# Cross attention: the weighing of key blocks 0 to 9 done two blocks at a time, and the maxima slots dealt out anew

## The chip, the cores and the metric

The kernel runs on one core of a Trainium2 chip. The metric is the device time of one execution in microseconds (us). The core has a matrix engine (TensorE, in profile rows PE, its weight loads PEld), a vector engine (VectorE, DVE), a scalar engine (ScalarE, ACT), a general engine (GpSimd, POOL) and a queue engine (SyncE, SP). Each works through its own list of instructions in order, and they wait for each other by semaphores.

## The reference

A decoder layer on x of 4 x 1024 x 512: self attention over 2048 fixed keys, cross attention over 1601 context rows with 16 heads of 32, and a feed-forward part with 8 experts. The change lies in the cross attention alone. Cut to that:

```python
q = _split_heads(Q @ Wq_w.T + Wq_b)
k = _split_heads(K @ Wk_w.T + Wk_b)
v = _split_heads(V @ Wv_w.T + Wv_b)
scores = jnp.einsum('bhqd,bhkd->bhqk', q, k) / np.sqrt(DK).astype(np.float32)
scores = jnp.where(mask == 0, jnp.float32(-1000000000.0), scores)
attn = jax.nn.softmax(scores, axis=-1)
out = jnp.einsum('bhqk,bhkd->bhqd', attn, v)
```

The softmax needs, for each query and head, the maximum of its scores over all 1601 keys.

## The kernel before

The cross attention is cut into 32 units: 4 batches x 4 groups of 4 heads x 2 halves of 512 queries. A unit goes through 13 key blocks (`kt` 0 to 12, 128 keys each, the last 65). Keys stand on the partitions and queries along the free dimension, so the maximum over keys can't be had from these scores. It is found one unit ahead in a second product with queries on the partitions: 64 slots a unit, each one matmul of 402 keys (`mx`, L1579, which calls L1096) into one of three PSUM banks (`mx_ps`), and one VectorE read of that bank that adds the mask and takes the maximum (`read`, L1756 on, which calls L1103). Slot n may be written once slot n-3 has been read: TensorE waits on `mx_read` ahead of every slot, VectorE on `mx_made`.

TensorE's order is written out by hand in `unit`. In block `kt` it makes the scores of block `kt`+1, for two pairs of heads (`score`, L1594, two matmuls; `add_mask`, L1600, one each), with slots strewn between; then two more slots; then it weighs block `kt` (`weigh`, L1608): the probabilities times the values, four heads at once in four column tiles of the array (32 columns each), two passes each, so 8 matmul records; then what is left of the block's slots. `SLOTS_OF` says how many slots each block has: blocks 0 to 8 share all 64. In block 9 (`TURN`) the finished maxima are turned by TensorE (L1584), copied by ScalarE and sent through DRAM into the next unit's queries as one more row. In block 12 TensorE also starts the sum of the probabilities (column tiles again, L1608 into `xa_mx_ps`), and behind block 12 `add_up` adds VectorE's and GpSimd's share of it.

ScalarE takes the exponential of each pair's scores (L1726); the scores of a pair may be overwritten once that is done, and block n's exponential goes into a ring of four places, so it waits until block n-4 has been weighed. GpSimd adds the probabilities of blocks 0 to 8 (L1561), VectorE those of 9 to 11 behind its 64 reads (L1778), then the reciprocal (L1782) and the product (L1786). The last of the 32 units has no slots, as no unit follows it.

Of the kernel before, what the change touches and what calls it, by code (L numbers as in the profile page):

```python
# [592 lines left out]
KT = (S2 + P - 1) // P  # L593
# [466 lines left out]
RING = 4  # L1060
# [334 lines left out]
def cross_attention(nc, ident, ident_b, kT, qT, v, mask_q, mask_t, row, oT, first, queries_1, probs, any_key, outputs, Wo, bo, x1):  # L1395
# [7 lines left out]

    HALF = S // BANK
    units = B * GROUPS * HALF
    SLOTS_OF = [2, 7, 8, 8, 8, 8, 8, 8, 7] + [0] * (KT - 9)
    SLOT_OF = [sum(SLOTS_OF[:n]) for n in range(KT + 1)]
    assert SLOT_OF[KT] == SLOTS
    TURN = 9
    OWN = {"pool": tuple(range(9)), "dve": (9, 10, 11)}  # L1410
    OWN_LAST = {"pool": tuple(range(5)), "dve": tuple(range(5, 12))}
    POOL_ADDS, DVE_ADDS = len(OWN["pool"]) - 1, len(OWN["dve"])
    FIRST_STORED = GROUPS * HALF
# [3 lines left out]
    with ExitStack() as ctx:  # L1417
# [8 lines left out]
        unread, maxima, neg_max, max_row = first.unread, first.maxima, first.neg_max, first.max_row  # L1426
# [31 lines left out]
        def keys_of(kt):  # L1458
            return LAST if kt == KT - 1 else P

        def wait_added(eng, u, kt, own):

            if kt < 0:
                u, kt, own = u - 1, kt + KT, OWN
            if kt == KT - 1:
# [32 lines left out]
        with nc.Block() as block:  # L1498
# [53 lines left out]
            def _(pool):  # L1552
# [5 lines left out]
                def add(u, kt, left, right):  # L1558
                    for pr in range(PAIRS):
                        pool.wait_ge(exped, PAIRS * (KT * u + kt) + pr + 2 + PAIRS)  # L1560
                        pool.tensor_tensor(sums[pr][:, :, :], left[pr][:, :, :],  # L1561
                                           right[pr][:, :, :], ALU.add).then_inc(pool_added, 1)

                def unit(u, par, half, at, more):
                    pool.wait_ge(total_made, u + 2)
                    add(u, 1, prob[at], prob[(at + 1) % RING])
                    own = OWN if more else OWN_LAST
                    for n, kt in enumerate(own["pool"][2:]):
# [7 lines left out]
            def _(pe):  # L1576
                def mx(u, par, half, slot):
                    m = SLOTS * u + slot
                    pe.wait_ge(mx_read, m + 2)  # L1579
                    scores_of_slot(pe, mx_ps[slot % 3], qp[par], kp[par], half, slot).then_inc(mx_made, 1)  # L1580

                def turn_peaks(u):
                    pe.wait_ge(peaks, u + 3)
                    pe.transpose(peak_ps[0:GH * QB, 0:P], neg_max[:, :], ident[:, :]).then_inc(row_made, 1)  # L1584

                def score(u, par, half, kt, pr):
                    keys = keys_of(kt)
                    if kt == 0 and pr == 0:
                        pe.wait_ge(row_in, 16 * (u + 1))
                    queries = slice(half * BANK, (half + 1) * BANK)  # L1590
                    pe.wait_ge(exped, PAIRS * (KT * u + kt - 1) + pr + 2 + PAIRS)
                    for jj in range(2):
                        j = 2 * pr + jj
                        pe.matmul(scores[pr][0:keys, jj, :], kp[par][0:ROWS97, j, kt * P:kt * P + keys],  # L1594
                                  qp[par][0:ROWS97, j, queries], start=True, stop=False)
# [9 lines left out]
                def four_heads(total, left, right, start, stop):  # L1605
                    for j in range(GH):
                        mine = slice(j * DK, (j + 1) * DK)
                        last = pe.matmul(total[mine, :], left(mine), right[j // 2][0:left(mine).shape[0], j % 2, :],  # L1608
                                         start=start, stop=stop, tile_position=(0, j * DK))
                    return last  # L1610

                def weigh(u, par, kt, ring):
                    keys = keys_of(kt)
                    if kt == 0:
                        pe.wait_ge(o_kept, u + 2)
                    pe.wait_ge(exped, PAIRS * (KT * u + kt + 1) + 1 + PAIRS)
                    if kt == KT - 1:
                        pe.wait_ge(sum_kept, u + 2)
                        four_heads(sum_ps, lambda mine: ones[0:keys, :], prob[ring], True, False)
                    four_heads(o_ps, lambda mine: vg[par][0:keys, kt, mine], prob[ring],  # L1620
                               kt == 0, kt == KT - 1).then_inc(weighed, 1)
# [30 lines left out]
                def unit(u, par, half, at, more):  # L1652
                    nxt = (par if half == 0 else 1 - par, 1 - half)
                    for kt in range(KT):
                        slots = iter(range(SLOT_OF[kt], SLOT_OF[kt + 1]) if more else ())

                        def maxima(most):
                            for slot in itertools.islice(slots, most):
                                mx(u + 1, *nxt, slot)

                        following = (u, par, half, kt + 1) if kt + 1 < KT else (u + 1, *nxt, 0) if more else None
                        between = 1 if kt else 0
                        for pr in range(PAIRS) if following else ():
                            score(*following, pr)
                            if pr == 1:
                                maxima(between)
                            add_mask(following[2], following[3], pr, 0)
                            if pr == 0:
                                maxima(between)
                            add_mask(following[2], following[3], pr, 1)  # L1670
                            if pr == 0:
                                maxima(between)
                        if more and kt == TURN:
                            turn_peaks(u + 1)
                        maxima(2 * between)
                        weigh(u, par, kt, (at + kt) % RING)
                        if more and kt == 0:
                            pe.wait_ge(row_kept, u + 3)
                            pe.wait_ge(sum_kept, u + 2)
                            if half == 1:  # L1680
                                pe.wait_ge(loaded, 16 * (LOADS * (u // HALF + 1)))
                        maxima(SLOTS_OF[kt])
                        if not more and kt < DC:
                            turn_output_weight(kt)
                    add_up(u, OWN if more else OWN_LAST)

# [13 lines left out]
            def _(act):  # L1700
# [28 lines left out]
                def unit(u, par, half, at, more):  # L1729
                    for kt in range(KT):  # L1730
                        if kt + 1 < KT:
                            exp(u, kt + 1, (at + kt + 1) % RING, OWN if more else OWN_LAST)
                        elif more:
                            exp(u + 1, 0, (at + KT) % RING, OWN)
                        if more and kt == TURN:
                            keep_row(u + 1)
# [1264 lines left out]
```

## Time and profile before

| what | value |
|---|---|
| median of 3 runs | 3894.85 us (3888.32 to 3895.75) |
| the profiled execution | span 3891.2 us |
| TensorE busy | 3788.4 us (97%) |
| VectorE busy | 2395.0 us (62%) |
| ScalarE busy | 1432.7 us (37%) |
| GpSimd busy | 1534.5 us (39%) |
| cross attention, from its first to its last unit | about 1288 to 3015 us |

The profiled execution gives only its span, from its first to its last instruction; no time of its own around the span is given, and the span lies between the lowest and the median of the runs, 3.7 us below the median. Times in rows are us from the span's start. Matmuls are pipelined: a busy TensorE is not one at its peak. The granted TensorE clock is 1.00 over the cross attention.

### The profile page before, as it was taken

The page shows a single profiled execution, that of the slowest core. Times are in us where ns is not written, and L with a number is a line of the kernel's source. Part 1 is how long each engine was busy: PE and PEld are TensorE (multiplying, and loading weights), DVE is VectorE, ACT ScalarE, POOL GpSimd, SP SyncE. Part 2 cuts the span into 40 slices and gives each one's busy share as a digit, 9 for nine tenths or more (in the row PEclk, how much of TensorE's full clock was granted, in tenths as well). Part 3 has the DMA queues.
Part 4 walks back from the last instruction along what each step waited for, and adds up shares of the span by engine and source line. Part 5 has one row for each costly group of instructions (what it writes and reads, how often), then busy time and mean ns, then how long its engine had stood idle before and what let it go on. Part 6 is the DMA issues. An engine that isn't in the chain of part 4 may idle for free. (4 is left out here: it accounts for less than half of the span.)

```text
span 3891.2 us, 63669 instructions
## 1 busy us (share of the span) xinstructions
PE 3788.4 (97%) x19001; PEld 2532.2 (65%) x19161; DVE 2395.0 (62%) x6222; ACT 1432.7 (37%) x1793; POOL 1534.5 (39%) x860
## 2 busy tenths in 40 slices
PE   8999999999999899999999999999999999999998
PEld 7888888888877444544444444544444777777776
DVE  6544444444458688888888788878887533433135
ACT  3111222233224455455545555445555221222332
POOL 1000000000013667766677666766665222312234
PEclk9999999999999999999999999999999999999999
DMA  4001000145555322222112222222111433328579
GB/s 157 32 32 32 32 32 32 44 172 178 191 179 186 94 57 55 57 57 46 35 38 57 58 57 58 54 57 55 33 36 49 151 126 132 114 92 278 185 263 332
DMA packets 223177, 381.89 MB, mean 98 GB/s; under 512 B 17544, under 2 KB 102056, under 8 KB 222892
## 3 DMA queue, kind: packets, MB, share of 16 engines
q1 hardware_dynamic: 192876, 301.34, 26.7%
q0 software_dynamic: 14752, 49.29, 3.5%
q10 hardware_dynamic: 15264, 27.79, 1.9%
q8 instruction: 137, 2.24, 0.2%
q14 instruction: 148, 1.21, 0.1%
HBM read 229.71 MB, written 148.66 MB: 97 GB/s over the span
## 5 line engine op out<-in xcount | busy, mean ns | idle before, releaser
L1103 DVE CUSTOM_DVE_ANT_0 xf_unread<-xa_mx_ps,mask_q 128x402 bf16<-128x402 f32 x1984 | 1036.0, 573 | 290.3 <-PE xa_mx_ps L1096 156.7
L1726 ACT ACTIVATE probs<-xa_scores 128x1024 f32<-128x1024 f32 (+1 forms) x416 | 417.5, 1024 | 417.0 <-PE xa_scores L1600 371.6
L1726 ACT ACTIVATE xa_probs<-xa_scores 128x1024 f32<-128x1024 f32 (+1 forms) x416 | 417.3, 1024 | 397.8 <-PE xa_scores L1600 355.1
L1561 POOL TENSOR_TENSOR xa_sums<-xa_sums,xa_probs 128x1024 f32<-128x1024 f32 x220 | 519.7, 2383 | 18.1 <-POOL xa_sums L1561 15.7
L1561 POOL TENSOR_TENSOR xa_sums<-xa_sums,probs 128x1024 f32<-128x1024 f32 x220 | 519.3, 2381 | 18.9 <-POOL xa_sums L1561 15.3
L1600 PE MATMUL xa_scores<-mask_t,ident_b 128*128 128x512 bf16 (+1 forms) x1505 | 499.7, 387 | 5.3 <-issue 0.2
L1096 PE MATMUL xa_mx_ps<-xa_kp,queries 96*128 96x402 f32 x1024 | 364.2, 418 | 0.8
L1096 PE MATMUL xa_mx_ps<-xf_kp,queries 96*128 96x402 f32 x960 | 341.5, 418 | 0.4
L1594 PE MATMUL xa_scores<-queries,xf_kp 97*128 97x512 f32 (+1 forms) x832 | 284.2, 423 | 16.3 <-ACTq L1748 8.2
L1096 PEld LDWEIGHTS xa_mx_ps<-xa_kp,queries 96*128 96x128 f32 x1024 | 181.7, 189 | 172.2 <-DVE xf_maxima L1103 111.6
L1594 PE MATMUL xa_scores<-queries,xa_kp 97*128 97x512 f32 (+1 forms) x832 | 284.7, 423 | 1.8 <-ACT probs L1726 1.8
L1600 PEld LDWEIGHTS xa_scores<-mask_t,ident_b 128*128 128x128 bf16 (+1 forms) x1664 | 122.9, 100 | 244.7 <-issue 212.0
L253 POOL TENSOR_TENSOR sa_rstd<-sa_var,sa_power 128x1 f32<-128x1 f32 x32 | 17.7, 552 | 662.6 <-DVE sa_var L440 662.6
L1096 PEld LDWEIGHTS xa_mx_ps<-xf_kp,queries 96*128 96x128 f32 x960 | 170.4, 189 | 157.1 <-DVE xf_maxima L1103 98.3
L386 ACT ACTIVATE sa_pT_high<-sa_pT_ps 128x512 fp32r<-128x512 f32 x128 | 73.1, 597 | 534.1 <-PE sa_pT_ps L305 534.1
L44 PE MATMUL sa_o_ps<-sa_v_high,sa_pT_high 128*128 128x512 f32 x512 | 209.3, 409 | 3.0 <-DVE sa_pT_low L465 3.0
L44 PE MATMUL sa_scores<-weights,sa_nT_high 128*128 128x512 f32 x512 | 204.4, 399 | 1.4 <-DVE sa_nT_low L448 1.4
L46 PE MATMUL sa_scores<-weights,sa_nT_low 128*128 128x512 f32 x512 | 203.2, 397 | 0.0
L1594 PEld LDWEIGHTS xa_scores<-queries,xf_kp 97*128 97x128 f32 (+1 forms) x832 | 148.8, 187 | 83.5 <-ACT xa_probs L1726 26.0
L45 PE MATMUL sa_scores<-queries,sa_nT_high 128*128 128x512 f32 x512 | 202.6, 396 | 0.0
L46 PE MATMUL sa_o_ps<-sa_v_high,sa_pT_low 128*128 128x512 f32 x512 | 201.2, 393 | 0.0
L45 PE MATMUL sa_o_ps<-sa_v_low,sa_pT_high 128*128 128x512 f32 x512 | 199.8, 390 | 0.0
(415 smaller groups left out, 7388.0 us busy)
## 6 DMA issues: line engine op xcount, KB each, us to landing
bridge_rows<-sorted_in SPq DMA_DIRECT2D x78, 256.0 KB
sorted_out<-ex_made ACTq DMA_DIRECT2D x78, 256.0 KB
queries<-qT_high SPq DMA_DIRECT2D x30, 512.0 KB
xf_kp<-kT_high SPq DMA_DIRECT2D x16, 800.5 KB, 12.4
xa_kp<-kT_high SPq DMA_DIRECT2D x16, 800.5 KB
rows<-in_ctx SPq DMA_DIRECT2D x16, 768.0 KB, 5.1
values<-cxl_v SPq DMA_DIRECT2D x48, 256.0 KB
kT_high<-cxl_kT_high SPq DMA_DIRECT2D x12, 768.0 KB, 4.0
```

What stands on the lines that cost most here:

```text
L44: pe.matmul(out, lh, rh, start=start, stop=False)
L45: pe.matmul(out, lh, rl, start=False, stop=False)
L46: return pe.matmul(out, ll, rh, start=False, stop=stop)
L253: pool.tensor_tensor(rstd[:, :], var[:, :], power[:, :], ALU.pow).then_inc(root, 1)
L386: act.activation(pT[0][:, j * KB:(j + 1) * KB, :], pT_ps[j % 2][:, :, :], ACT.Copy).then_inc(pT_high, 1)
L1096: return pe.matmul(out[:, 0:MKEYS], qp[0:MAXROW, j, first:first + P], kp[0:MAXROW, j, MFIRST[kb]:MFIRST[kb] + MKEYS], start=True, stop=True)
L1103: return dve.tensor_tensor_reduce(out=unread[slot % 2][:, :], in0=scores[:, 0:MKEYS], in1=mask_q[:, half * QB + qt, MFIRST[kb]:MFIRST[kb] ...
L1561: pool.tensor_tensor(sums[pr][:, :, :], left[pr][:, :, :], right[pr][:, :, :], ALU.add).then_inc(pool_added, 1)
L1594: pe.matmul(scores[pr][0:keys, jj, :], kp[par][0:ROWS97, j, kt * P:kt * P + keys], qp[par][0:ROWS97, j, queries], start=True, stop=False)
L1600: last = pe.matmul(scores[pr][0:keys, jj, :], ident_b[0:keys, 0:keys], mask_t[0:keys, kt, queries], start=False, stop=True)
L1726: act.activation(prob[ring][pr][0:keys, :, :], scores[pr][0:keys, :, :], ACT.Exp, scale=SCALE).then_inc(exped, 1)
```

## The change

Two things change, both in the order of TensorE's instructions; no instruction of the computation is added or left out.

- Blocks 0 to 9 are no longer weighed in their own block, but in twos in the odd block: 0 and 1 in block 1, and so on to 8 and 9 in block 9. Blocks 10, 11 and 12 stay as they were. The waits at the head of `weigh` go with it, the wait for `o_kept` from block 0 to block 1.
- The slots are dealt 3, 8, 7, 9, 7, 9, 7, 9, 5 instead of 2, 7, 8, 8, 8, 8, 8, 8, 7, and the second pair's two mask products have a slot between them, as the first pair's already had.

```diff
@@ -1403,10 +1403,11 @@
     HALF = S // BANK
     units = B * GROUPS * HALF
-    SLOTS_OF = [2, 7, 8, 8, 8, 8, 8, 8, 7] + [0] * (KT - 9)
+    SLOTS_OF = [3, 8, 7, 9, 7, 9, 7, 9, 5] + [0] * (KT - 9)
...
     TURN = 9
+    WEIGHED_AT = {1: (0, 1), 3: (2, 3), 5: (4, 5), 7: (6, 7), 9: (8, 9), 10: (10,), 11: (11,), 12: (12,)}
@@ -1665,15 +1666,15 @@
                             if pr == 1:
                                 maxima(between)
                             add_mask(following[2], following[3], pr, 0)
-                            if pr == 0:
-                                maxima(between)
+                            maxima(between)
                             add_mask(following[2], following[3], pr, 1)
                             if pr == 0:
                                 maxima(between)
                         if more and kt == TURN:
                             turn_peaks(u + 1)
                         maxima(2 * between)
-                        weigh(u, par, kt, (at + kt) % RING)
+                        for due in WEIGHED_AT.get(kt, ()):
+                            weigh(u, par, due, (at + due) % RING)
```

What that does to TensorE's list stands at two places. The first is the end of block 0, between the last mask product of block 1's scores and the first slots (`xa_mx_ps` is a slot's bank, `xa_o_ps` the weighed sum). Before:

```order
L1600 MATMUL xa_scores<-mask_t,ident_b 128x512 x2
L1615 REGISTER_ALU
L1616 ISA [waits xa_o_kept]
L1608 MATMUL xa_o_ps<-probs,xf_vg 32x512 [waits xa_exped]
L1608 MATMUL xa_o_ps<-probs,xf_vg 32x512 x3
L1678 REGISTER_ALU
L1579 ISA [waits xa_sum_kept,xa_row_kept]
L1096 MATMUL xa_mx_ps<-xf_kp,queries 128x402 [waits xa_mx_read]
```

Now:

```order
L1601 MATMUL xa_scores<-mask_t,ident_b 128x512 x2
L1679 REGISTER_ALU
L1680 REGISTER_ALU [waits xa_row_kept]
L1580 ISA [waits xa_sum_kept]
L1096 MATMUL xa_mx_ps<-xf_kp,queries 128x402 [waits xa_mx_read]
```

The weighing of block 0 is gone from here, so a unit's first slot stands right behind the scores. The second place is the weighing in block 3, with the slots ahead of it and behind. Before:

```order
L1096 MATMUL xa_mx_ps<-xf_kp,queries 128x402 [waits xa_mx_read]
L1616 ISA
L1608 MATMUL xa_o_ps<-xa_probs,xf_vg 32x512 [waits xa_exped]
L1608 MATMUL xa_o_ps<-xa_probs,xf_vg 32x512 x3
L1579 REGISTER_ALU
L1096 MATMUL xa_mx_ps<-xf_kp,queries 128x402 [waits xa_mx_read]
```

Now:

```order
L1096 MATMUL xa_mx_ps<-xf_kp,queries 128x402 [waits xa_mx_read]
L1617 REGISTER_ALU
L1609 MATMUL xa_o_ps<-xa_probs,xf_vg 32x512 [waits xa_exped]
L1609 MATMUL xa_o_ps<-xa_probs,xf_vg 32x512 x3
L1617 ISA
L1609 MATMUL xa_o_ps<-xa_probs,xf_vg 32x512 [waits xa_exped]
L1609 MATMUL xa_o_ps<-xa_probs,xf_vg 32x512 x3
L1580 REGISTER_ALU
L1096 MATMUL xa_mx_ps<-xf_kp,queries 128x402 [waits xa_mx_read]
```

Two weighings, of blocks 2 and 3, now stand back to back between two slots; block 2 has slots alone.

## Rows read from the trace of the kernel before

**Rows 1.** The page: engines; costliest groups (busy, mean ns, idle before, releaser).

```profile
span 3891.2 us, 63669 instructions
PE 3788.4 (97%) x19001; PEld 2532.2 (65%) x19161; DVE 2395.0 (62%) x6222; ACT 1432.7 (37%) x1793; POOL 1534.5 (39%) x860
L1103 DVE CUSTOM_DVE_ANT_0 xf_unread<-xa_mx_ps,mask_q 128x402 bf16<-128x402 f32 x1984 | 1036.0, 573 | 290.3 <-PE xa_mx_ps L1096 156.7
```

**Rows 2.** Windows of one unit: its slots' reads, then the rest.

```profile
core 0: us, PE busy (x) PEld busy (x) DVE busy (x) ACT busy (x) POOL busy (x), PEclk, DMA share, GB/s
1562.27:1599.62 37.35, 37.16 (x192) 20.31 (x195) 33.48 (x128) 16.46 (x17) 36.03 (x16) 1.00 0.00 1
1599.62:1612.20 12.58, 12.51 (x77) 4.11 (x76) 11.34 (x11) 8.46 (x10) 0.37 (x1) 1.00 0.00 1
```

**Rows 3.** VectorE's timeline in block 8 of that unit (start, us).

```profile
1597.02 0.58 DVE L1103 CUSTOM_DVE_ANT_0 xf_unread<-xa_mx_ps,mask_q 128x402 bf16<-128x402 f32 x1
...
1597.52 0.57 DVE L1103 CUSTOM_DVE_ANT_0 xf_unread<-xa_mx_ps,mask_q 128x402 bf16<-128x402 f32 x1
...
1598.62 0.58 DVE L1103 CUSTOM_DVE_ANT_0 xf_unread<-xa_mx_ps,mask_q 128x402 bf16<-128x402 f32 x1 [0.51 <-issue]
```

**Rows 4.** TensorE's timeline in block 5 of the unit before.

```profile
1526.56 0.63 PE L1594 MATMUL xa_scores<-queries,xf_kp 97*128 97x512 f32 x2
...
1528.85 0.75 PE L1096 MATMUL xa_mx_ps<-xf_kp,queries 96*128 96x402 f32 x2
1529.53 1.06 PE L1608 MATMUL xa_o_ps<-probs,xf_vg 128*32 128x512 f32 x8
1530.53 0.82 PE L1096 MATMUL xa_mx_ps<-xf_kp,queries 96*128 96x402 f32 x3
1531.18 0.63 PE L1594 MATMUL xa_scores<-queries,xf_kp 97*128 97x512 f32 x2
```

**Rows 5.** TensorE's timeline, from block 12 of one unit into block 0 of the next.

```profile
1555.88 1.06 PE L1608 MATMUL xa_mx_ps<-probs,xa_ones 65*32 65x512 f32 x8
1556.76 1.04 PE L1608 MATMUL xa_o_ps<-probs,xf_vg 65*32 65x512 f32 x8
1557.62 1.04 PE L1608 MATMUL xa_mx_ps<-xa_sums,xa_ones 128*32 128x512 f32 x8
1558.59 0.73 PE L1594 MATMUL xa_scores<-queries,xf_kp 97*128 97x512 f32 x2
...
1560.09 0.61 PE L1600 MATMUL xa_scores<-mask_t,ident_b 128*128 128x512 bf16 x2
1560.62 1.07 PE L1608 MATMUL xa_o_ps<-probs,xf_vg 128*32 128x512 f32 x8
1561.62 0.64 PE L1096 MATMUL xa_mx_ps<-xa_kp,queries 96*128 96x402 f32 x2
```

**Rows 6.** TensorE's timeline from block 8 to the unit's end.

```profile
1597.99 0.63 PE L1096 MATMUL xa_mx_ps<-xa_kp,queries 96*128 96x402 f32 x2
...
1600.29 0.27 PE L1584 MATMUL xa_mx_ps<-ident,xf_neg_max 128*16 128x128 f32 x1
1600.49 1.06 PE L1608 MATMUL xa_o_ps<-xa_probs,xf_vg 128*32 128x512 f32 x8
1601.48 0.73 PE L1594 MATMUL xa_scores<-queries,xf_kp 97*128 97x512 f32 x2
...
1612.18 0.72 PE L1594 MATMUL xa_scores<-queries,xa_kp 97*128 97x512 f32 x2
```

**Rows 7.** ScalarE's timeline in block 7 of that unit.

```profile
1596.70 1.03 ACT L1726 ACTIVATE xa_probs<-xa_scores 128x1024 f32<-128x1024 f32 x1 [0.33 <-PE xa_scores L1600]
```

**Rows 8.** VectorE's timeline behind the unit's reads.

```profile
1599.73 0.22 DVE L1768 TENSOR_REDUCE xf_neg_max<-xf_maxima 128x16 f32<-128x64 f32 x1
...
1610.92 0.69 DVE L1786 TENSOR_TENSOR any_key<-xa_o_sb,xa_sum_sb 128x512 f32<-128x512 f32 x1
```

**Rows 9.** Line 1584 over the whole trace, one instruction a unit with slots.

```profile
L1584 PE MATMUL xa_mx_ps<-ident,xf_neg_max x31: 272/273/273, 1330.1 to 2957.7; 128*16 128x128 f32 x31
```

## The prediction

> **What bounds the kernel now.** I read the page first: TensorE is busy 97% of the span [rows 1], which would say that anything that shortens its work shortens the kernel. But a matmul that waits or drains counts as busy, so I went to one unit. The windows [rows 2] part it into the stretch in which VectorE reads the 64 slots (37.35 us) and the rest (12.58 us, no slots). TensorE looks full in both. The timeline of VectorE [rows 3] shows how the first stretch is paced. Reads that follow each other at once start 0.50 us apart (1597.02, 1597.52). The next one starts 1.10 us later, at 1598.62: that is 0.60 us in which VectorE had nothing to read, and it lies beside a weighing. So 64 reads take 64 x 0.50 = 32.0 us, and 37.35 - 32.0 = 5.35 us are gaps. Eight weighings lie in the stretch (blocks 1 to 8); 8 x 0.60 = 4.8 us, nearly all of it.
>
> The reason is the three banks. While TensorE weighs it makes no slots; VectorE lives on what lies in the banks, at most three reads, partly used up when the weighing starts.
>
> Is TensorE or VectorE the limit there? TensorE's prices, from its timelines: of a block's four score and four mask products the first six take 1558.59 to 1560.09 [rows 5], 1.50 us; 0.10 of that is getting out of the weighing before (two score products behind a weighing show 0.73 us, elsewhere 0.63 [rows 4, 5]), so one takes 0.233 and eight 1.87 us. The weighing starts 0.53 us after the last two began, 0.06 more than they need: getting into the column tiles. Three slots take 1530.53 to 1531.18 with the 0.10 in it, 0.18 to 0.19 each [rows 4]. A lone weighing then costs 1561.62 - 1560.62 = 1.00 [rows 5], plus 0.06 and 0.10: 1.16 us. Two blocks with 16 slots are 3.74 + 3.04 + 2.32 = 9.10 us of TensorE's own work. VectorE needs 16 x 0.50 + 2 x 0.60 = 9.20. Measured are 2 x (1531.18 - 1526.56) = 9.24 [rows 4]. The two chains are nearly even, and VectorE's is the longer one. That is the fact on which the forecast rests.
>
> **The change, part by part.** All per unit with slots, of which there are 31 [rows 9]; their mean length is (2957.7 - 1330.1) / 30 = 54.3 us.
>
> *What TensorE saves.* Three weighings already stand in a row, in block 12: they start 0.88 and 0.86 us apart, the next other matmul 0.97 behind the last [rows 5]. A second weighing in a pair so costs 0.87 instead of 1.16, 0.29 less. Five pairs: 1.45 us a unit of TensorE's work. It is a gain only where TensorE is the limit.
>
> *Block 0.* Its weighing leaves the place ahead of the first slot, so the stretch of reads begins 1.16 us earlier. VectorE is free then: its last work of the unit before ends at 1611.61 [rows 8], before the unit's end at 1612.18 [rows 6], and the first read would fall 2.5 us into the next. **-1.16.** It could be as little as -1.0, if the wait for the copied sum, which stands here, bites.
>
> *The stretch of reads.* It holds four pairs (0+1 to 6+7) where it held eight lone weighings. Once VectorE has emptied the banks, each further us of weighing is a further us of gap: a pair's gap is 0.60 + 0.87 = 1.47 us. 4 x 1.47 - 8 x 0.60 = +1.08. The other bound: in an even block TensorE now has only 1.87 + 7 x 0.19 = 3.2 us of work against 3.5 of reads. So it comes to the pair held up by VectorE at every slot, and with less in the banks than before; I allow up to 0.1 us a gap for that (an estimate; 0.10 is what a matmul that had to start afresh lost above): 4 x 1.57 - 4.8 = +1.48. I take **+1.25**, between the two. Check by the two chains, for two blocks with 16 slots: TensorE 3.74 + 3.04 + 2.03 = 8.81, VectorE 8.0 + 1.47 to 1.57 = 9.5. VectorE's is now the longer by 0.7, against 0.1 before, and two blocks grow from 9.24 to about 9.5.
>
> *Block 9.* Block 8 has neither weighing nor its last two slots behind one, and the weighing of 8 comes in block 9, behind the last read, where TensorE alone is the limit: **+0.87** (as a lone weighing inside the stretch it is one of the eight gaps above).
>
> *ScalarE at block 9.* The scores of block 10 may overwrite a pair once block 9's exponential of it is done: 1.03 us [rows 7], begun when its last mask product is finished, 0.61 - 0.23 = 0.4 us after that one starts [rows 5]. In between TensorE now has two scores, two masks and three slots, 7 matmuls or 1.5 us, then goes on at once, where a weighing used to cover it. **+0.25**, an estimate between 0 and 0.4.
>
> *Hidden, and what hides them.* The maxima are reduced 0.11 us after the last read [rows 8] and wanted at 1600.29, 2.3 us behind the last slots [rows 6]; the new order leaves the same eight matmuls between. Without that cover it would be some 0.2. The new maximum row has 0.87 us more before it is wanted. No DMA is added, and SP and POOL's lists stay. Blocks are still weighed before the ring needs their place: block n's exponential asks for block n-4. GpSimd's 16 additions fill 36 of 37 us of the stretch [rows 2] and begin with block 1's exponentials, which don't move; VectorE's additions follow them, and end well before block 12's sum. The slot that now parts the second pair's masks changes only which matmul stands where: nothing.
>
> *The last unit* has no slots, so TensorE is its limit: -1.45 us once.
>
> Sum: -1.16 + 1.25 + 0.87 + 0.25 = +1.21 us a unit; x 31 = +37.5; -1.45: **+36 us**. For the profiled execution that is a span of 3891.2 + 36 = 3927; the median of the runs lies 3.7 above that span, so 3894.85 + 36 = **3931**. Bounds: with every term at its lower end -1.16 + 1.08 + 0.87 + 0 = +0.79, or +23 us; at the upper -1.0 + 1.48 + 0.87 + 0.4 = +1.75, or +53.
>
> **A page weighed against the rows.** In rows, leaving and entering the column tiles loses TensorE 0.29 us each time [rows 5], and saving it in five places would give the first rival below. The Trainium skill, "TensorEngine Tiling (Array Packing)", Key Properties, states the same: changing the tiling mode drains the array. By that rule alone the change is a gain. The same page's section PSUM Bottleneck says that tiling speeds up the array but not the evacuation of PSUM, which may become the limit; the gaps of [rows 3] lie on that side.
>
> **The rivals.**
> - *TensorE is the limit after all* (faster). Then the 1.45 us come back whole in all 32 units: -46 us, 3849. For it: 97% busy, and chains only 0.1 us apart before. Against: VectorE's 0.60 gap at each weighing can't shrink when the weighing gets longer. The point from which it decides: if VectorE had four reads (2.0 us) banked when a pair begins, not the three that the banks allow. Chance 6%.
> - *The pairs' longer gaps are made up for elsewhere* (no change). The small gaps (5.35 - 4.8 = 0.55 us), and an exponential that is in time take 0.25: 1.21 - 0.55 - 0.25 = +0.4 us a unit, and +11 us in all; for no change at all (within 8 us) block 0 must give more than its 1.16 as well. Chance 8%, 6% of it within 8 us.
> - *ScalarE becomes a wait in every odd block*, not in block 9 alone, since each even block lacks the weighing that covered its exponential: 0.3 us in four more places, 1.2 x 31 = 37 us more, 3968. Against: in those blocks VectorE holds TensorE up for longer than that. Chance 6%.
> - *The forecast*, 23 to 53 us slower: 80%.
>
> **How the numbers follow.** The likeliest case gives 3931. Its bounds are 3918 and 3948; I go down to 3906, where the second rival's +11 us lies, and leave out both far rivals and the last of the upper bound: 3906 to 3947. A measurement of this kernel can tell about 0.2% (8 us) from no change. Slower by more than that: the forecast, the third rival, and the rest of the second, 0.87; within it 0.06; faster 0.07.
>
> **What the changed profile would show.** First read of a unit about 2.5 us after the unit's first score product, not 3.7. Four gaps of about 1.5 us (read starts 2.0 us apart) in each unit, none of 0.6 beside blocks 2, 4, 6 and 8. Two blocks (4 and 5) of 9.5 us or more, with weighings 0.87 apart. Block 9 longer by 0.9 to 1.2. Units of some 55 us. Wrong would be the forecast if the gaps at pairs stayed under 1.2 us, or if a unit came out at 52.5.

## The result, and the profile after

The changed kernel is slower: 3952.09 us (median of 4 runs, 3947.16 to 3953.09) against 3895.3 us (4 runs, 3888.32 to 3898.31), a ratio of 1.0151 [1.0136, 1.0165], or +57 us. The forecast of 3931 had the sign, and the mechanism of the undisturbed unit; the time lies 5 us above the range. The profiled execution took 3947.16 us, its span is 3945.0 us, so between the two spans +53.8 us are to be explained.

From the page: totals, and VectorE's reads of the slots.

```profile
span 3945.0 us, 63662 instructions
PE 3828.4 (97%) x19001; PEld 2541.8 (64%) x19161; DVE 2372.7 (60%) x6222; ACT 1436.3 (36%) x1793; POOL 1529.8 (39%) x860
L1103 DVE CUSTOM_DVE_ANT_0 xf_unread<-xa_mx_ps,mask_q 128x402 bf16<-128x402 f32 x1984 | 1017.8, 572 | 370.7 <-issue 194.1
```

The counts of instructions, and the mean read of some 0.57 us, are those of [rows 1]. TensorE is at 97% again, with 40 us more of "busy" for the same 19,001 matmuls: time in which they stood in the pipeline. What moved is the idle time ahead of VectorE's reads, 290.3 to 370.7 us: +80.4 us, or 2.6 us a unit. Of that, 18 us only changed sides, from busy to idle (the reads' busy time went from 1036.0 to 1017.8 us for the same 1984 reads); the other 62 us are longer gaps, in the undisturbed units and at the six places below.

Windows of a unit with slots, its reads and then the rest (the columns are those of [rows 2]):

```profile
1570.32:1609.03 38.71, 38.37 (x190) 20.16 (x193) 32.95 (x128) 17.09 (x17) 37.39 (x16) 1.00 0.00 1
1609.03:1622.85 13.82, 13.74 (x86) 4.67 (x86) 11.34 (x11) 8.62 (x10) 0.19 (x1) 1.00 0.06 20
```

The reads take 38.71 us where they took 37.35 [rows 2], 1.36 more; by medians over the 31 units, from the first read's start to the last one's, 36.97 became 38.21, 1.24 more. VectorE's timeline at a pair, blocks 4 and 5 of the unit before:

```profile
1537.88 0.57 DVE L1103 CUSTOM_DVE_ANT_0 xf_unread<-xa_mx_ps,mask_q 128x402 bf16<-128x402 f32 x1
...
1538.37 0.57 DVE L1103 CUSTOM_DVE_ANT_0 xf_unread<-xa_mx_ps,mask_q 128x402 bf16<-128x402 f32 x1
...
1540.37 0.58 DVE L1103 CUSTOM_DVE_ANT_0 xf_unread<-xa_mx_ps,mask_q 128x402 bf16<-128x402 f32 x1 [1.42 <-issue]
```

The three banks are empty after the read of 1538.37, and the next read starts 2.00 us later: a gap of 2.00 - 0.50 = 1.50 us, where a lone weighing left 0.60 [rows 3]. The other side, TensorE's timeline over blocks 4 and 5 (the first row is block 4's start, the last one block 6's):

```profile
1530.68 0.63 PE L1595 MATMUL xa_scores<-queries,xf_kp 97*128 97x512 f32 x2
...
1534.56 0.63 PE L1595 MATMUL xa_scores<-queries,xf_kp 97*128 97x512 f32 x2
...
1537.89 1.92 PE L1609 MATMUL xa_o_ps<-probs,xf_vg 128*32 128x512 f32 x16
1539.75 0.82 PE L1096 MATMUL xa_mx_ps<-xf_kp,queries 96*128 96x402 f32 x3
1540.41 0.63 PE L1595 MATMUL xa_scores<-queries,xf_kp 97*128 97x512 f32 x2
```

The two weighings cost 1539.75 - 1537.89 = 1.86 us in a row, 0.86 to 0.87 for the second one as forecast. Yet the two blocks take 1540.41 - 1530.68 = 9.73 us, against 9.24 [rows 4]: TensorE gains 0.29 and the pair of blocks loses 0.49. Even blocks take 3.88 us, not TensorE's own 3.2 (an estimate of the forecast): the reads hold them up, as the run with short reads below shows.

TensorE's timeline from a unit's start to the next one's:

```profile
1567.84 0.73 PE L1595 MATMUL xa_scores<-queries,xf_kp 97*128 97x512 f32 x2
...
1607.97 0.62 PE L1595 MATMUL xa_scores<-queries,xf_kp 97*128 97x512 f32 x2
...
1610.27 1.06 PE L1609 MATMUL xa_o_ps<-probs,xf_vg 128*32 128x512 f32 x8
1611.15 1.04 PE L1609 MATMUL xa_o_ps<-xa_probs,xf_vg 128*32 128x512 f32 x8
1612.12 0.73 PE L1595 MATMUL xa_scores<-queries,xf_kp 97*128 97x512 f32 x2
...
1622.83 0.72 PE L1595 MATMUL xa_scores<-queries,xa_kp 97*128 97x512 f32 x2
```

The unit takes 1622.83 - 1567.84 = 54.99 us; before it was 1612.18 - 1558.59 = 53.59 [rows 5, 6]. Medians over the units, from the start of each block's scores to the next one's, in us (an average unit whose blocks are all undisturbed, 53.63 before and 54.98 after, summed from unrounded medians):

| blocks | 0+1 | 2+3 | 4+5 | 6+7 | 8 | 9 | 10 to 12 |
|---|---|---|---|---|---|---|---|
| before | 7.82 | 9.15 | 9.24 | 9.24 | 4.44 | 3.03 | 10.70 |
| after | 8.29 | 9.55 | 9.71 | 9.68 | 2.88 | 4.16 | 10.71 |
| slots before, after | 9, 11 | 16, 16 | 16, 16 | 16, 16 | 7, 5 | 0 | 0 |

31 units at +1.35 us make +42 us. That leaves 12 of the 54. The 31 units with slots together take 1743.0 us where they took 1682.1, +60.9; the part ahead of them is 3.8 shorter, the last unit 1.8 longer (45.8 to 47.5, to the end of its last sum), the part behind it 5.0 shorter. So some 19 us more than the undisturbed units' +42 were lost inside the units. They are at six places, where the loop over units jumps back to its start (every fourth unit): there, blocks 12, 0 and 1 are longer than their medians by 16.2 us in all before, by 37.1 us after (other blocks gave 2 us back). The forecast has no term for this.

**A turn of the loop.** ScalarE's timeline, before, and then after, at the first turn, between the last copy of unit 3 and the first exponential of unit 4:

```profile
1503.40 0.60 ACT L1745 ACTIVATE xa_sum_sb<-xa_mx_ps 128x512 f32<-128x512 f32 x1 [0.26 <-PE xa_mx_ps L1608]
1506.79 1.02 ACT L1726 ACTIVATE probs<-xa_scores 128x1024 f32<-128x1024 f32 x1 [2.79 <-PE xa_scores L1600]
```

```profile
1505.09 0.60 ACT L1746 ACTIVATE xa_sum_sb<-xa_mx_ps 128x512 f32<-128x512 f32 x1 [0.26 <-PE xa_mx_ps L1609]
1512.04 1.94 ACT L1727 ACTIVATE probs<-xa_scores 128x1024 f32<-128x1024 f32 x2 [6.35 <-issue]
```

ScalarE came back 2.99 us after its jump before, and 6.55 us after it now (from the jump, a record of the trace at 1503.47 and at 1505.16, to ScalarE's next record, a register instruction 0.33 us ahead of the exponential). `<-issue` says that it waited for nothing that the profile shows. TensorE waits for it:

```profile
1506.26 0.72 PE L1595 MATMUL xa_scores<-queries,xf_kp 97*128 97x512 f32 x2 [1.24 <-issue]
...
1508.01 0.90 PE L1096 MATMUL xa_mx_ps<-xf_kp,queries 96*128 96x402 f32 x3
1513.12 1.22 PE L1595 MATMUL xa_scores<-queries,xf_kp 97*128 97x512 f32 x2 [4.21 <-ACT probs L1727]
```

What differs is what SyncE has put in the DMA queues by then. Its list at this place, before and after:

```profile
1502.71 0.37 SPq L1515 DMA_DIRECT2D oT<-any_key  x1
1503.43 0.86 SPq L1068 DMA_DIRECT2D xa_kp<-kT_high  x2
```

```profile
1503.21 0.37 SPq L1516 DMA_DIRECT2D oT<-any_key  x1
1504.43 0.96 SPq L1068 DMA_DIRECT2D xa_kp<-kT_high  x2
```

The loads of the next heads' keys and values (800.5, 800.5, 768.0 and 32.5 KB, the first of them twice) begin 0.04 us ahead of ScalarE's jump before (0.04 to 0.06 at the six turns), 0.73 us ahead of it now (0.73 to 0.74). The profile has instruction queues beside the data queues (packets, MB, share of the 16 engines). The changed kernel from the jump on (1505.2 to 1509.5, then 1509.5 to 1510.5):

```profile
q1 hardware_dynamic: 145, 0.87, 95.0%
...
q1 hardware_dynamic: 42, 0.20, 99.7%
q14 instruction: 1, 0.01, 3.8%
```

The packet of instructions, 4.45 us after the jump, comes behind 0.87 MB of keys; before, it came 0.92 us after the jump. The second turn is like the first. At the four later turns of this execution ScalarE was back in 2.5 to 3.0 us, and TensorE itself was late at its own jump (2.55 to 2.79 us of `<-issue`, where it was 0.95 to 1.56 at all six turns before), and at three of them once more in the midst of block 1's weighing. At unit 12:

```profile
1964.00 0.73 PE L1595 MATMUL xa_scores<-queries,xf_kp 97*128 97x512 f32 x2 [2.71 <-issue]
...
1969.97 1.91 PE L1609 MATMUL xa_o_ps<-probs,xf_vg 128*32 128x512 f32 x12
1973.47 1.05 PE L1609 MATMUL xa_o_ps<-probs,xf_vg 128*32 128x512 f32 x4 [1.60 <-issue]
```

Part of the loss at the turns is TensorE's clock. TensorE's last slot before its wait ends at 1508.91, and the next product starts at 1513.12. In that wait the granted clock falls to 0.50, the lower of its two levels (1.2 instead of 2.4 GHz), and stays there into block 1 (the clock is the third number from the end):

```profile
1511.90:1518.70 6.80, 5.58 (x14) 3.27 (x14) 2.34 (x8) 3.29 (x4) 5.38 (x3) 0.50 1.03 203
1513.12:1521.17 8.05, 8.05 (x33) 4.16 (x34) 3.42 (x12) 2.91 (x3) 7.85 (x4) 0.66 1.08 226
```

The second row is block 1 of unit 4: no wait of TensorE's lies in it, and it takes 8.05 us against a median of 5.82. The same happens at the second turn and, from the wait of 2.79 us at TensorE's jump on, at the sixth: 20.5 us at the lower level in three stretches, in which the blocks without another wait lose 2.2, 2.4 and 3.0 us. So some 7.7 of the 21 us that the turns lose more than before are work at the lower clock, and nearly all of the rest is standing still. In the kernel before, the clock falls at none of its six turns.

### The profile page after: what moved, and what is told of

Read it like the earlier page. It is cut to its first block and busy times, and to the rows that moved or that the text cites. A ratio compares the mean times of both kernels' runs of the same rounds, so it can differ in the third digit from the quotient of the medians.

```text
span 3945.0 us, 63662 instructions
## 1 busy us (share of the span) xinstructions
PE 3828.4 (97%) x19001; PEld 2541.8 (64%) x19161; DVE 2372.7 (60%) x6222; ACT 1436.3 (36%) x1793; POOL 1529.8 (39%) x860
## 3 DMA queue, kind: packets, MB, share of 16 engines
q14 instruction: 148, 1.21, 0.1%
## 5 line engine op out<-in xcount | busy, mean ns | idle before, releaser
L1103 DVE CUSTOM_DVE_ANT_0 xf_unread<-xa_mx_ps,mask_q 128x402 bf16<-128x402 f32 x1984 | 1017.8, 572 | 370.7 <-issue 194.1
L1601 PE MATMUL xa_scores<-mask_t,ident_b 128*128 128x512 bf16 (+1 forms) x1505 | 540.0, 392 | 2.6 <-issue 0.2
L1096 PE MATMUL xa_mx_ps<-xa_kp,queries 96*128 96x402 f32 x1024 | 404.3, 449 | 5.3
L1096 PE MATMUL xa_mx_ps<-xf_kp,queries 96*128 96x402 f32 x960 | 383.8, 454 | 5.1
L1601 PEld LDWEIGHTS xa_scores<-mask_t,ident_b 128*128 128x128 bf16 (+1 forms) x1664 | 143.1, 100 | 302.6 <-issue 276.3
L1595 PE MATMUL xa_scores<-queries,xf_kp 97*128 97x512 f32 (+1 forms) x832 | 286.7, 426 | 30.3 <-issue 13.1
L1096 PEld LDWEIGHTS xa_mx_ps<-xa_kp,queries 96*128 96x128 f32 x1024 | 190.2, 191 | 126.1 <-DVE xf_maxima L1103 106.0
L1096 PEld LDWEIGHTS xa_mx_ps<-xf_kp,queries 96*128 96x128 f32 x960 | 180.9, 194 | 117.6 <-DVE xf_maxima L1103 94.3
## 6 DMA issues: line engine op xcount, KB each, us to landing
xf_kp<-kT_high SPq DMA_DIRECT2D x16, 800.5 KB, 12.7
xa_kp<-kT_high SPq DMA_DIRECT2D x16, 800.5 KB
rows<-in_ctx SPq DMA_DIRECT2D x16, 768.0 KB, 5.0
kT_high<-cxl_kT_high SPq DMA_DIRECT2D x12, 768.0 KB, 4.0
```

Of the source, the lines that this page charges most:

```text
L1096: return pe.matmul(out[:, 0:MKEYS], qp[0:MAXROW, j, first:first + P], kp[0:MAXROW, j, MFIRST[kb]:MFIRST[kb] + MKEYS], start=True, stop=True)
L1103: return dve.tensor_tensor_reduce(out=unread[slot % 2][:, :], in0=scores[:, 0:MKEYS], in1=mask_q[:, half * QB + qt, MFIRST[kb]:MFIRST[kb] ...
L1601: last = pe.matmul(scores[pr][0:keys, jj, :], ident_b[0:keys, 0:keys], mask_t[0:keys, kt, queries], start=False, stop=True)
```

## The experiments

Two things are to be told apart. In the undisturbed unit: that VectorE's reads through three banks set the pace (the prediction's theory), against a cost of the pairs on TensorE itself. At the turns: that the key loads, now further ahead of the jump, hold up the instructions, against a longer jump for a reason of the code or of the chip. "Units" below are sums of median blocks, and "turns" the excess of blocks 12, 0 and 1 at the six turns, as above. Where one time is given without a range, the kernel was timed once; a few us between two such times say nothing.

### Shorter reads, in both kernels

```diff
 MB, MKEYS = 4, 402
+READ = 134
...
-        out=unread[slot % 2][:, :], in0=scores[:, 0:MKEYS],
-        in1=mask_q[:, half * QB + qt, MFIRST[kb]:MFIRST[kb] + MKEYS], scale=1.0, scalar=LOWEST,
+        out=unread[slot % 2][:, 0:READ], in0=scores[:, 0:READ],
+        in1=mask_q[:, half * QB + qt, MFIRST[kb]:MFIRST[kb] + READ], scale=1.0, scalar=LOWEST,
```

VectorE reads a third of each bank, so the maxima are those of a third of the keys; TensorE's list is as it was. In the kernel before:

> The kernel before, with VectorE reading only the first 134 of a slot's 402 columns, so that its reads are about 0.22 us apart instead of 0.50 (the maxima are then taken over a third of the keys; everything TensorE does stays). This is the base for the run of the changed kernel with the same cut. Theory 1 (VectorE's reads out of three banks set the pace beside the weighings): a unit shrinks from 53.6 us by about 0.7, to some 52.9. Theory 2 (TensorE's own work is all that counts there): 53.6 stays.

In the changed kernel:

> The changed kernel with the same cut of the reads. Theory 1 (the added time is VectorE starved at the pairs): with short reads VectorE is never behind, and the change loses its cost: a unit of 52.3 to 52.9 us, at or below that of the kernel before with the same cut. Theory 2 (the added time comes from TensorE or ScalarE, say from waits for the exponential in blocks without a weighing): the changed kernel stays 1.4 us a unit slower, some 54.3 or more.

Measured: 3862.01 and 3843.99 us, beside 3896.59 for the kernel before, each timed once. Units of 52.97 and 52.36 us, both as expected of VectorE's reads as the limit: with short reads the changed order is the faster one, by 0.6 us a unit, and by 18 us in all. A unit of each, TensorE's timeline, first of the kernel before and then of the changed one:

```profile
1550.31 0.73 PE L1595 MATMUL xa_scores<-queries,xf_kp 97*128 97x512 f32 x2
...
1603.24 0.72 PE L1595 MATMUL xa_scores<-queries,xa_kp 97*128 97x512 f32 x2
```

```profile
1598.97 0.72 PE L1596 MATMUL xa_scores<-queries,xa_kp 97*128 97x512 f32 x2
...
1651.27 0.72 PE L1596 MATMUL xa_scores<-queries,xa_kp 97*128 97x512 f32 x2
```

52.93 and 52.30 us. The sign of the change turns with the length of the reads alone, so a cost of the pairs on TensorE is out: VectorE's reads are the limit. Of TensorE's 1.45 us a unit only 0.6 comes out even so. The three pairs 2+3 to 6+7 bring 0.1 us each (9.03 to 9.05 us for two blocks became 8.94), not 0.29: even with short reads the even block takes 3.36 us, above TensorE's own 3.2. And block 9 is as long as with full reads (4.17). Part of the rest is the forecast's own term for ScalarE, which the rows of block 9 show (further below); for the even blocks the cause was not measured.

### The two parts of the change, each alone

Pairs without the new slots, as an edit to the changed kernel:

```diff
-    SLOTS_OF = [3, 8, 7, 9, 7, 9, 7, 9, 5] + [0] * (KT - 9)
+    SLOTS_OF = [2, 7, 8, 8, 8, 8, 8, 8, 7] + [0] * (KT - 9)
...
-                            maxima(between)
+                            if pr == 0:
+                                maxima(between)
```

> Pairs of weighings as in the change, slots as before. Theory 1 (VectorE starved at each pair, and the longer the more slots lie in blocks that can't feed it): the pairs alone bring the whole cost, and the moved slots give some of it back: a unit of 55.3 to 56.0 us, against 55.0 of the full change and 53.6 before. Theory 2 (the moved slots are the cost): a unit near 53.6.

The new slots with every block weighed in its own place, as an edit to the changed kernel:

```diff
-                        for due in WEIGHED_AT.get(kt, ()):
-                            weigh(u, par, due, (at + due) % RING)
+                        weigh(u, par, kt, (at + kt) % RING)
```

> Slots moved as in the change, each block weighed alone as before. Theory 1: slots and weighings must be in step, since a block with nine slots and a weighing asks more of VectorE than a block has time for: slower than before too, a unit of 54.2 to 55.7 us. Theory 2 (only the pairs matter): 53.6.

Measured: 3990.22 us (units 55.48, turns 52.8) and 3965.46 us (units 55.44, turns 35.6). Each part alone is worse than both together (54.98). The new deal of slots does suit the pairs: it saves 0.5 us a unit of what they cost, 0.4 of it in blocks 2 to 7; why is not shown by a run. Without pairs it costs, in odd and in even blocks: 4.97 us for an odd block of nine slots and one weighing, 4.6 to 4.75 for an even one of seven. In both kernels the turns are as bad as in the changed one, also without any pair (ScalarE back 6.4 to 8.6 and 5.5 to 8.2 us after its jump, with the loads 0.73 us ahead). So the pairs are not what lengthens the jump; what all three share is how far ahead of it the loads go out.

### The key loads two blocks later

```diff
-                        sp.wait_ge(weighed, u * KT + 1 + RING)
+                        sp.wait_ge(weighed, u * KT + 3 + RING)
```

SyncE issues the loads at a turn not when the last block of the unit before has been weighed, but some two blocks into the new one. In the changed kernel, and in the kernel before:

> The changed kernel, with the loads of the next group's keys, values and queries held back until two more blocks are weighed (a larger number in one wait of SyncE). Its trace shows TensorE standing still 18 us longer than before at the six turns of the loop over units, where ScalarE's jump back takes 6.6 to 6.9 us in the first two. Theory B (the fetch of ScalarE's and TensorE's instructions stands behind the load that SyncE now issues 0.7 us ahead of the jump): ScalarE's jump back takes 2.5 to 3 us in every turn, the 30 us of extra stalls in blocks 0 and 1 go, clean units stay at 55.0 us; 3915 to 3930 us. Theory C (the longer list of instructions of the changed loop is the cause): nothing changes, 3945 to 3955.

> The kernel before with the same one number changed. Theory B: the stalls in blocks 0 and 1 behind the turns (9 us in six turns) go, 3882 to 3890 us, faster than the kernel before by 0.15 to 0.35%. Theory C: 3890 to 3898, no difference.

Measured: 3910.64 us (3908.26 to 3911.87), 1.009 [1.0074, 1.0107] times the kernel before on the same chip, which took 3874.32 us (17 runs); and 3872.29 us (12 runs), 0.999 [0.9981, 0.9999]. Units 55.00 and 53.61, as without the edit; turns 11.7 and 9.5. The kernel before gains 0.1% by it, less than the 0.15 to 0.35% expected, and its interval ends just short of no change. ScalarE at the first turn of the changed kernel with late loads:

```profile
1506.70 0.60 ACT L1746 ACTIVATE xa_sum_sb<-xa_mx_ps 128x512 f32<-128x512 f32 x1 [0.26 <-PE xa_mx_ps L1609]
1509.52 1.94 ACT L1727 ACTIVATE probs<-xa_scores 128x1024 f32<-128x1024 f32 x2 [2.23 <-PE xa_scores L1601]
```

and SyncE there:

```profile
1504.80 0.37 SPq L1516 DMA_DIRECT2D oT<-any_key  x1
1516.31 1.65 SPq L1068 DMA_DIRECT2D xa_kp<-kT_high  x2
```

The load starts at 1516.31, long after ScalarE is back (2.43 us after its jump, and 2.4 to 2.7 at all six turns). Since this was another chip than the first, one on which the kernel before took 21 us less, the 41 us between 3952.09 and 3910.64 are no measure. So both ran once more, side by side:

> The changed kernel unaltered, on the same chip as the next run, since the kernel before itself was 21 us apart between two chips. Theory B: about 13 to 30 us above the changed kernel with late loads, the difference all in blocks 0 and 1 behind the loop's turns and ScalarE's jumps back of up to 7 us; 1.2 to 1.6% over the kernel before. Theory C: the same time as with late loads.

> The changed kernel with late loads once more, beside the unaltered one: theory B 0.9% over the kernel before, as on the other chip; theory C the same time as the run above.

Measured: 3937.77 us (3934.01 to 3941.11), 1.0153 [1.0138, 1.0169], and 3912.04 us (3908.59 to 3914.37), 1.0092 [1.0076, 1.0107], with the kernel before at 3877.55 us (11 runs). The change costs the same 1.5% on both chips, and the later loads take 26 us of it away, with units equal at 55.00, and turns of 43.4 and 10.0 (33 us, as the two profiled executions are 32 us apart). The lower clock goes with them: 30.7 us of it at the six turns with the early loads, none there with the late ones. The place of the loads is thus the cause of the turns' loss. The rest, +35 us, is close to the forecast's +36, but not the same sum: the units cost 31 x 1.37 = +43, turns shorter than those of the profiled kernel before (10.0 against 16.2) give some 6 back, and what is left lies elsewhere. With late loads in both kernels the change costs 3910.64 - 3872.29 = +38 us.

### Pairs in one place only

The kernel before with its own slots, and pairs in one place; the loop over `WEIGHED_AT` is that of the change. Blocks 2 and 3, in the midst of the reads:

```diff
+    WEIGHED_AT = {2: (), 3: (2, 3), **{kt: (kt,) for kt in (0, 1, *range(4, 13))}}
...
-                        weigh(u, par, kt, (at + kt) % RING)
+                        for due in WEIGHED_AT.get(kt, ()):
+                            weigh(u, par, due, (at + due) % RING)
```

> The kernel before with one pair alone: blocks 2 and 3 weighed together in block 3, slots as before. Theory 1 (each pair in the stretch of reads costs VectorE a gap longer by the second weighing): a unit of 53.9 to 54.3 us, against 53.6, with blocks 2 and 3 together longer by 0.3 to 0.7 and all other blocks within 0.1. Theory 2 (pairs save TensorE 0.29 each): 53.3.

Blocks 9 and 10, and 11 and 12, where there are no slots:

```diff
+    WEIGHED_AT = {**{kt: (kt,) for kt in range(9)}, 10: (9, 10), 12: (11, 12)}
```

> The kernel before with pairs where no slots are: blocks 9 and 10 weighed in block 10, 11 and 12 in block 12. VectorE's reads have no part in it. If TensorE's own work is all that counts there, a unit loses 2 x 0.29 = 0.6 us (53.0). If ScalarE's two exponentials of a block (2.0 us and some 0.5 us on either side) can't keep up with a block of scores without a weighing (1.9 us), the saving goes into waits for them: 53.5 to 53.9 us.

Blocks 0 and 1, where VectorE has nothing to read yet:

```diff
+    WEIGHED_AT = {0: (), 1: (0, 1), **{kt: (kt,) for kt in range(2, 13)}}
```

> The kernel before with blocks 0 and 1 alone weighed together in block 1. Theory 1: the reads begin 1.16 us earlier and cost one gap longer by the second weighing (0.9 us) in the same stretch: a unit 0.1 to 0.4 us shorter, 53.2 to 53.5. Theory 2 (any pair in the stretch costs as much as that of blocks 2 and 3, 0.6 us): 54.2.

Measured, each kernel timed once, against the kernel before on the same chip: 3887.97 us (3874.32, whose runs reach from 3867.58 to 3883.57), 3880.19 us (same chip, within those runs) and 3869.05 us (3877.55, 3873.33 to 3883.76).

The pair in the midst costs 0.57 us a unit by medians: blocks 2 and 3 take 4.34 + 5.38 = 9.72 us, and took 9.15. TensorE's timeline of one such block 3 and the next start:

```profile
1571.12 0.62 PE L1595 MATMUL xa_scores<-queries,xf_kp 97*128 97x512 f32 x2
...
1573.97 1.06 PE L1609 MATMUL xa_o_ps<-xa_probs,xf_vg 128*32 128x512 f32 x8
1574.85 1.04 PE L1609 MATMUL xa_o_ps<-probs,xf_vg 128*32 128x512 f32 x8
...
1576.48 0.63 PE L1595 MATMUL xa_scores<-queries,xf_kp 97*128 97x512 f32 x2
```

5.36 us for a block that took 4.63. All three units came out as expected of VectorE's and ScalarE's limits (54.20, 53.82, 53.40). The pair in blocks 0 and 1 gains: 2.30 + 5.28 = 7.58 us against 7.82. The sum of the forecast's terms for it is -1.16 + 0.87 = -0.29. The pairs at the end save nothing, though TensorE alone was thought the limit there: blocks 9 to 12 take 2.19 + 3.89 + 2.22 + 5.60 = 13.9 us against 13.7. TensorE's waits there for the exponentials, over the cross attention (us in total, times, longest), with the two pairs:

```profile
PEld xa_scores L1595 <- ACT probs L1728: 55.1, 90, 2.7
PEld xa_scores L1595 <- ACT xa_probs L1728: 39.6, 78, 0.8
```

and in the kernel before:

```profile
PEld xa_scores L1594 <- ACT probs L1726: 45.0, 54, 2.7
PEld xa_scores L1594 <- ACT xa_probs L1726: 40.3, 48, 0.9
```

66 such waits more: a block that has neither slots nor a weighing gives TensorE 1.87 us of work, and ScalarE needs two exponentials of 1.02 us for it.

### The pair that gains, with the late loads

To the edits of the last two parts one of the slots comes on top: one more in block 0, where there is now time, and one less in block 7.

```diff
-    SLOTS_OF = [2, 7, 8, 8, 8, 8, 8, 8, 7] + [0] * (KT - 9)
+    SLOTS_OF = [3, 7, 8, 8, 8, 8, 8, 7, 7] + [0] * (KT - 9)
```

> What the runs point to: blocks 0 and 1 alone in a pair, one slot moved from block 7 to block 0, and the late loads. Theories 1 and B together: a unit of 53.2 to 53.4 us (-7 to -12 us in 31 units) and fewer stalls at the turns (-2 to -9): 0.25 to 0.55% faster than the kernel before.

Measured: 3864.42 us (7 runs, 3862.22 to 3869.61), 0.9969 [0.9958, 0.998] times the kernel before. It beats both, by 13 and by 73 us. Units of 53.32 us, against 53.63. What each of its three edits gives was not timed apart; by units, the pair has 0.23 of the 0.31 us (53.40 with it alone).

## Why the prediction was right in sign and short in size

- **VectorE is the limit of the stretch of reads**: shown. With short reads the change becomes a gain. The rival "TensorE is the limit after all" is out. With it goes the rule in Key Properties of the Trainium skill's page "TensorEngine Tiling (Array Packing)", that a change of the tiling mode drains the array, as a forecast by itself. What the Trainium skill says in PSUM Bottleneck on that page, that the evacuation of PSUM may become the limit, fits the gaps of 1.50 us. TensorE's saving itself is real (0.86 to 0.87 for a second weighing), but three banks hold at most 1.5 us of reads, and a pair takes 1.86.
- **Block 0, -1.16**: -1.20 measured. The unit's first read is at 1570.32, 2.48 us after its first score product, where it was 1562.27 - 1558.59 = 3.68.
- **The stretch of reads, +1.25** (1.08 to 1.48): +1.36 measured in the unit shown, +1.24 by medians. Gaps of 1.50 us at most pairs, as forecast at 1.47 to 1.57 (1.30 at two of the four in some units, the one shown among them; of the eight gaps before, two were 0.38 in such units). The two blocks "of about 9.5" are 9.70: 16 x 0.50 + 1.50 = 9.50, and 0.2 of small gaps, which TensorE in the even block, without its weighing, did not take away.
- **Block 9, +0.87 and +0.25**: together +1.13 (3.03 to 4.16). The rows of the weight loads tell the two apart: the second pair's scores wait for ScalarE and start 1.08 us after the block, where they started 0.73 us after it (1599.19 - 1598.46), so that ScalarE's term is some 0.3. With the pairs alone, where block 8 is not cut short, block 9 takes 3.89, which is the +0.86 of the weighing and nothing more.

```profile
1609.04 0.30 PEld L1595 LDWEIGHTS xa_scores<-queries,xf_kp 97*128 97x128 f32 x2 [0.50 <-ACT xa_probs L1727]
```

- **A unit, +1.21**: +1.35 by medians. The second rival's set-offs did not show, and the third rival, ScalarE in every odd block, did not either: the odd blocks' growth is VectorE's gap. x 31 gives +42 us against +37.5.
- **The last unit, -1.45**: +1.8 in these two traces. But between executions its length is either 45.6 to 46.0 or 47.2 to 47.5 us, whatever the order; on the lower level it is 45.8 before and 45.9 after. So it gained nothing, and no run was made on why; ScalarE's pace, as in the pairs at the end, would explain it, but that is only argued.
- **The step that failed** is in the part "Hidden, and what hides them": "No DMA is added, and SP and POOL's lists stay". It is true of the lists and wrong of the times; the forecast put the turns at nothing, without a reason. At each of six turns the loads of the next keys were issued 0.04 to 0.06 us ahead of ScalarE's jump before and 0.73 us or more ahead after; the next instructions of ScalarE, or of TensorE, came behind them, TensorE's clock fell in three of the waits, and blocks 12, 0 and 1 lost 21 us more than before. Later loads alone took 26 us back, to a ratio of 1.0092. That forecast + this term, 3931 + 21 = 3952, is just the time measured is luck: the units cost 4 us more than forecast and the last unit 3 more, and the parts ahead of the units and behind them, in which nothing was changed, were 9 us shorter in the profiled execution.

Why the loads came earlier against the jump can be read from the traces. SyncE's load stands behind its store of a finished piece, and the store waits for VectorE's product. In us against ScalarE's jump (minus is ahead of it; the first two columns are medians over the six turns):

| kernel | last read ends | product ends | first load issued | ScalarE back after |
|---|---|---|---|---|
| before | -12.7 | -0.95 | -0.06 to -0.04 | 2.8 to 3.7 |
| changed, two executions | -13.9 | -2.17 | -0.74 to -0.73 | 2.5 to 8.0 |
| pairs alone | -13.7 | -1.90 | -0.74 to -0.73 | 6.4 to 8.6 |
| slots alone | -14.0 | -2.18 | -0.74 to -0.73 | 5.5 to 8.2 |
| pairs at the end | -12.9 | -1.13 | -0.24 to -0.20 | 4.4 to 5.0 |
| pair 2+3 | -12.7 | -0.95 | -0.06 to -0.02 | 2.6 to 3.5 |
| pair 0+1 | -12.7 | -0.75 | +0.14 to +0.19 | 2.7 to 3.5 |
| before, short reads | -13.1 | -0.30 | +0.59 to +0.63 | 2.6 to 2.9 |
| changed, short reads | -14.4 | +0.34 | +1.23 to +1.25 | 2.4 to 2.7 |

The load goes out 0.9 us behind the product's end, but not sooner than 0.73 us ahead of the jump, when block 12 has been weighed. The product ends some 11.8 us behind the last read or 11.6 us behind GpSimd's last addition, whichever is later (the latter with pair 0+1 and with short reads). So in the changed kernel what counts is the work that TensorE has between the last read and the jump: block 8's weighing now lies there, and 12.7 us became 13.9. (With the slots alone it is block 8's two slots fewer that end the reads sooner.) It is not the length of a unit: pair 2+3 makes units 0.57 us longer, and its loads and jumps are those of before. The two columns on the right go together over these nine kernels: loads that go out 0.2 us ahead of the jump already cost ScalarE some 1.5 us. That it is the loads was tested by the late loads alone; the chain ahead of them is read off, not tested.

Whether ScalarE or TensorE is hit varies between executions: two of ScalarE's six jumps are long in the one profile of the changed kernel, five in the other; at the other five turns TensorE's own wait at its jump was 2.55 to 2.83 us. The traces show what goes with it. At those seven turns SyncE's second load was issued no later than 0.22 us after the jump; at the other five it was 0.97 us or later, and there ScalarE was back within 3 us. What holds the second load back at some turns stays open.

## What to carry to other kernels

Before merging stretches of one engine's work to save its changeovers, ask how long the engine that it feeds can live on what is buffered: here three banks held 1.5 us of reads, a pair of weighings took 1.9, and the merge paid only where nothing was being read. An engine that is busy 97% of the time by the page may still be paced by another; two chains of a block summed from rows tell. And where a loop jumps back, look at which large transfers are issued just ahead of the jump: when the work near the iteration's end changes, so can that order. A wait that such a load causes can cost twice, once as the wait and once more as TensorE's lower clock behind it.

## What was not expected of the hardware

- An engine's jump back to the start of a loop cost ScalarE 2.4 to 3.0 us where the large loads came some blocks later, and up to 8.6 us where 3.2 MB of loads were begun 0.7 us ahead of it (5.3 to 8.0 at the seven turns of the changed kernel that were hit). The packet on the instruction queue came 0.9 to 1.4 us after the jump in the one case, 3.2 to 6.5 us in the other where ScalarE was hit (3.2 to 5.8 at the seven turns). In the kernel before, one of six turns was slightly hit (3.73 us, its packet after 2.1).
- The same loads can hold up an engine well behind the jump: TensorE stood for 1.60 us in the midst of block 1's weighing with `<-issue`. The kernel before has such waits at a weighing too (4, of 4.3 us together), its version with late loads has none.
- The granted clock fell to 0.50 (1.2 GHz) for 3.4 or 6.8 us in or behind waits of TensorE at the turns: in nine of the changed kernel's twelve, after waits of 2.66 to 5.92 us, in none of the kernel before (waits of up to 1.56 us). It is no sharp line: with late loads it fell at single turns whose longest wait was 1.50 to 1.58 us, and waits of 2.55 to 2.71 us passed without a fall.
- The same kernel before took 3895 us on one chip and 3874 to 3878 us on two others, 0.5%, while the ratio of the change was 1.0151 and 1.0153.
